# Perceiver kernel, stage 9: the 16-head cross attention two heads at a time, in two groups of 64 rows

## The reference

```python
q = split_heads(hidden_states @ q_w.T + q_b)      # 16 heads of 16 channels
k = split_heads(context @ k_w.T + k_b)            # 4096 keys
v = split_heads(context @ v_w.T + v_b)
scores = einsum('bhqd,bhkd->bhqk', q, k) / sqrt(16)
scores = where(mask, -inf, scores)
probs = softmax(scores, axis=-1)
ctx = einsum('bhqk,bhkd->bhqd', probs, v)         # heads side by side, no output product
x = x + ctx
```

## Time and profile before

| | us |
|---|---|
| median of 3 runs | 1701.7 (1700.82 to 1702.98) |
| the profiled execution | 1701.72 |
| its span in the trace | 1699.9 |
| stage 9 in it, from its first instruction to the first product of stage 10 | about 927 to 1413 |
| from the first score of stage 9 to its last sum | 962.4 to 1408 |

### The profile page before, as it was taken

The page is one execution under the profiler, slowest core; times in us unless marked ns, Lnnn a source line. Parts: engine busy times, 40 slices in busy tenths (PEclk is TensorE's granted clock), DMA queues, the critical chain, the costliest instruction groups (busy, mean ns, idle before and its releaser), DMA issues.

```text
span 1699.9 us, 21512 instructions
## 1 busy us (share of the span) xinstructions
PE 1570.8 (92%) x8708; PEld 951.9 (56%) x8708; DVE 812.7 (48%) x1515; ACT 624.1 (37%) x1177; POOL 139.7 (8%) x181
## 2 busy tenths in 40 slices
PE   7998899999999999998989799999999998678698
PEld 3676554454677554676545355555555554444597
DVE  5543530003433433333632566777788863755432
ACT  1222321012342323333422466666667773103111
POOL 0001200001000301001010412102210000000000
PEclk9999899999999999999999999999999999778699
DMA  9024133200035201122131554547654315100050
GB/s 377 16 99 160 61 106 112 74 22 17 3 105 197 64 0 33 50 98 92 42 149 30 111 90 87 99 78 194 179 91 70 60 18 211 50 1 1 1 198 13
DMA packets 40133, 147.04 MB, mean 86 GB/s; under 512 B 6073, under 2 KB 21689, under 8 KB 30777
## 3 DMA queue, kind: packets, MB, share of 16 engines
q1 hardware_dynamic: 40034, 145.67, 29.8%
HBM read 123.08 MB, written 22.56 MB: 86 GB/s over the span
## 4 chain that ended last, share of the span: by engine, by line
PE 85%; DVE 7%; ACT 5%; issue 2%; DMA 1%; SPq 0%; DVEq 0%; ACTq 0%
PE PS L157 53%; PE PS L1767 7%; PE PS L1744 7%; PE PS L1699 6%; PE PS L559 2%; PE PS L1188 2%; ACT AR L1851 1%; PE PS L1365 1%; PE PS L1198 1%; PE PS L1758 1%; PE PS L2192 1%; PE PS L2128 1%; ACT CT L1411 1%; DVE SM L2224 1%; ACT L261 1%
## 5 line engine op out<-in xcount | busy, mean ns | idle before, releaser
L1784 DVE TENSOR_REDUCE SM<-PS 128x1 f32<-128x1024 f32 x256 | 308.6, 1221 | 104.5 <-PE PS L1699 103.3
L157 PE MATMUL PS<-CN,AR 128*128 128x256 f32 x768 | 180.5, 379 | 0.0
L157 PE MATMUL PS<-CT,HT 128*128 128x512 f32 x384 | 176.5, 593 | 2.0 <-ACT HT L663 2.0
L157 PE MATMUL PS<-HT,AR 128*128 128x512 f32 x328 | 160.5, 642 | 15.1 <-ACT HT L331 10.4
L157 PEld LDWEIGHTS PS<-CN,AR 128*128 128x128 f32 x768 | 143.6, 190 | 43.9 <-issue 28.7
L1744 PE MATMUL PS<-AR 99*128 99x256 bf16 x1024 | 161.5, 275 | 6.4 <-ACT CN L410 2.4
L1699 PE MATMUL PS<-AR 97*128 97x512 bf16 x512 | 152.9, 380 | 4.3 <-DMA AR<-rows 2.8
L157 PE MATMUL PS<-AR 128*128 128x512 f32 (+3 forms) x472 | 149.2, 471 | 7.0 <-DVE AR L594 2.5
L1851 ACT ACTIVATE AR<-PS 128x512 f32<-128x512 f32 x256 | 138.1, 597 | 25.8 <-PE PS L1744 25.8
L1744 PEld LDWEIGHTS PS<-AR 99*128 99x128 bf16 x1024 | 79.0, 97 | 109.7 <-issue 35.9
L157 PEld LDWEIGHTS PS<-AR 128*128 128x128 f32 x472 | 85.3, 196 | 71.0 <-issue 53.5
(11 more groups left out here) (310 smaller groups left out, 1936.6 us busy)
## 6 DMA issues: line engine op xcount, KB each, us to landing
CN<-ctx_n SPq DMA_DIRECT2D x24, 1024.0 KB, 4.8
AR<-k_parts SPq DMA_DIRECT2D x192, 128.0 KB
k_parts<-CN SPq DMA_DIRECT2D x32, 384.0 KB, 5.9
CN<-pack SPq DMA_DIRECT2D x6, 2048.0 KB, 7.3
v_ones<-CN SPq DMA_DIRECT2D x32, 288.0 KB, 3.4
CT<-ctx_t SPq DMA_DIRECT2D x8, 1024.0 KB, 19.2
AR<-pack SPq DMA_DIRECT2D x16, 512.0 KB, 3.7
AR<-pack SPq DMA_DIRECT2D x3, 2048.0 KB, 7.3
```

The costliest lines, as they stand in the source:

```text
L157: last = te.matmul(o, l, r, start=first and k == 0, stop=final and k == n - 1, skip_group_check=True)
L1784: ve.tensor_reduce(MX9[:, n % 2, u // 4, u % 4:u % 4 + 1], PS[:, b:b + 2, :].rearrange("p a b -> p (a b)"), AX, ALU.max).then_inc(*dv.inc( ...
```

## The change

It is confined to stage 9 and to where stages 10 and 11 keep their buffers (CT and CN change places).

- The unit is a **pair** of heads: one head in rows 0 to 63, the other in rows 64 to 127. The six products are in two groups of rows: M, 49 rows per head (parts 0·0, 1·0, mask, 0·1), and R, 50 rows per head (0·1 or 2·0 and so on, and the two parts of the maximum). `QQ9[:, pair, 0]` and `KM9` hold M, `QQ9[:, pair, 1]` and `KR_9` hold R.
- `best` multiplies the M rows alone: 2 matmuls of 512 columns over 49 rows for one head. A score needs two matmuls that add up, M and then R.
- 16 pairs x 8 groups = 128 groups; a group does what two steps did. `best_beside` issues a head's `best` between the score matmuls of the other head, twice per group; `both` issues the scores of both heads of the next step in alternation, and takes its two banks before its first matmul. A group then is: 2 x `best_beside`, `both`, the mixes of the group before. `best` runs 10 groups (20 reductions) ahead, where it ran 12 steps ahead.
- `PT9` has 6 buffers. `finish` and `turn_rows` come once per pair; on VectorE the two copies of `turn_rows` stand between the two reductions of the next group.
- The 27 jobs come whole, one at the end of a group. The fetches are 12 to 16 transfers per pair, M rows 3 pairs ahead into 4 buffers and R rows 2 pairs ahead into 3; those of pair 0's M rows are issued in stage 8. The values of the second batch take the place of the first's.

```diff
+        AHEAD = 10
...
+            for u in range(2 * AHEAD):
+                if u in (0, 2, 6, 10):
+                    yield "select", (0, 2, 6, 10).index(u), 0
+                if u > 2 and u % 2 and jobs:
                     yield ("job", *jobs.pop(0))
...
+        def pair_steps():
+            for g in range(128):
+                p, k = g // 8, g % 8
+                yield "score", g, 0
+                if g:
+                    yield "mix", g - 1, 0
+                if g in PAIR_JOBS:
+                    yield ("job", *PAIR_JOBS[g])
+                if k == 2 and p:
+                    yield "finish", p - 1, 0
+                if k == 5 and p < 15:
+                    yield "best_rows", p + 1, 0
+                if k == 6 and p < 15:
+                    yield "turn_rows", p + 1, 0
...
+            def score_bank(p, s, e):
+                b, before = SR9.take(("st", 9, p, s, e), ("e", 9, p, s, e))
+                pe.wait_ge(*before, ("kr", p), ("mrow", 9, p))
+                return b
...
+            def best_beside(g, e, p, s):
+                b, bs = best_bank(g, e), score_bank(p, s, 1 - e)
                 for y in range(2):
+                    z = best(g, e, b, y)
+                    score(p, s, 1 - e, bs, y, 0)
+                    last = score(p, s, 1 - e, bs, y, 1)
+                z.then_inc(*pe.inc("best", "best_ps", 9, g, e))
+                last.then_inc(*pe.inc("score", "st_ps", 9, p, s, 1 - e))
+
+            def both(p, s):
+                ba, bb = score_bank(p, s, 0), score_bank(p, s, 1)
+                for y in range(2):
+                    score(p, s, 0, ba, y, 0)
+                    score(p, s, 1, bb, y, 0)
+                    a = score(p, s, 0, ba, y, 1)
+                    b = score(p, s, 1, bb, y, 1)
...
                 if what == "score":
+                    p, s = n // 8, 2 * (n % 8)
+                    if n + AHEAD < 128:
+                        best_beside(n + AHEAD, 0, p, s)
+                        best_beside(n + AHEAD, 1, p, s)
+                    else:
+                        both(p, s)
+                    both(p, s + 1)
...
+            for what, n, k in pair_steps():
+                if what == "score":
+                    if n + AHEAD < 128:
+                        best(n + AHEAD, 0)
+                    if rows is not None:
+                        turn_rows(rows)
+                        rows = None
+                    if n + AHEAD < 128:
+                        best(n + AHEAD, 1)
```

More of the change, by code:

```diff
@@ L1649, in start_steps @@
                     yield "best_rows", 0, 0
-                if u == 9:
+                if u == 17:
                     yield "turn_rows", 0, 0
             assert not jobs
[L1654 to L1680, removed]
@@ L1703, in turn_rows, with best_bank @@
-            def turn_rows(n):
-                b, before = SR9.take(("rows", n), ("mrow", 9, n))
-                pb = PS[:, b, 0:128].bitcast(BF16)
[L1706 to L1714, removed]
+            def best_bank(g, e):
+                b, before = BP9.take(("best", 9, g, e), ("best", 9, g, e))
+                pe.wait_ge(*before, ("km", g // 8), ("qm", g // 8 % 8))
+                return b
@@ new lines, in score @@
+            def score(p, s, e, b, z, rest):
+                _, pr, cols = of_pair(p)
+                rows, keys = (R_ROWS[e], KR_9[p % 3]) if rest else (M_ROWS[e], KM9[p % 4])
+                c = 2 * s + z
+                return te.matmul(PS[:, b, z * 256:z * 256 + 256], keys[rows, c * 128:c * 128 + 128],
+                                 QQ9[rows, pr, rest, cols], start=not rest, stop=bool(rest), skip_group_check=True)
+            def best_beside(g, e, p, s):
+                b, bs = best_bank(g, e), score_bank(p, s, 1 - e)
+                for y in range(2):
+                    z = best(g, e, b, y)
[3 more added lines that the diff above has]
+                last.then_inc(*pe.inc("score", "st_ps", 9, p, s, 1 - e))
@@ L1715, in select @@
+            def select(n):
+                m, kind = n // 2, n % 2
+                got = [PB4.take(("sel", kind, 4 * m + k), ("qr" if kind else "qm", 4 * m + k)) for k in range(4)]
+                pe.wait_ge(*[p for _, before in got for p in before], ("p0", 9, "q", m), ("p1", 9, "q", m),
+                           ("p2", 9, "q", m) if kind else None)
+                parts = ((2, 2), (3, 1), (4, 0)) if kind else ((0, 0), (1, 1))
+                for c, (piece, part) in enumerate(parts):
                     for k, (b, _) in enumerate(got):
@@ L1732, in pe_9 @@
                 if what == "best":
-                    best(n, k)
+                    b = best_bank(n, k)
+                    best(n, k, b, 0)
+                    best(n, k, b, 1).then_inc(*pe.inc("best", "best_ps", 9, n, k))
                 if what == "turn_rows":
                     turn_rows(n)
-            for what, n, k in head_steps():
+            for what, n, k in pair_steps():
                 if what == "score":
[L1738 to L1751, removed]
+                    p, s = n // 8, 2 * (n % 8)
[5 more added lines that the diff above has]
+                    both(p, s + 1)
+                if what == "job":
+                    job_pe(pe, SR9, n, k)
                 if what == "turn_rows":
@@ L1803, in dve_9, with turn_rows @@
+            def turn_rows(p):
+                _, pr, cols = of_pair(p)
+                dv.wait_ge(("row_ps", 9, p), ("qr", pr))
+                for e in range(2):
+                    r = slice(64 * e + 32, 64 * e + 34)
+                    ve.tensor_copy(QQ9[r, pr, 1, cols], bank("rows", p)[:, 0:128].bitcast(BF16)[r, :]).then_inc(
+                        *dv.inc("turn", "mrow", 9, p))
             turn_out(dv, 9, "ht", HT, 0)
@@ L1807, in dve_9 @@
                 split_d_dve(dv, (9, "q", m), QP9[:, 0, m, :], RT9[m])
[L1808 removed]
+            rows = None
+            for what, n, k in start_steps():
                 if what == "best":
```

346 lines of the change are left out of this document (196 added, 150 removed).

## The result

| | before | after |
|---|---|---|
| median, us | 1701.77 (1700.82 to 1702.98), 4 runs | 1739.17 (1736.24 to 1743.42), 4 runs |
| ratio after / before | | 1.0221, 95% interval 1.0199 to 1.0244 |
| profiled execution, its span | 1701.72, 1699.9 | 1739.7, 1737.9 |
| first exponential of stage 9 | 963.75 | 977.41 |
| last sums matmul of stage 9 | 1407.48 | 1446.68 |

Of the 38.0 by which the spans differ, 1.1 arise before stage 9, 12.6 in its start, 25.5 between the first exponential and the last sums, and 1.2 are given back behind them. So the start came out nearly as forecast (+11.5), and the loop did not (+3.0 by the terms of the prediction).

What follows compares the result with a forecast made beforehand. TensorE was taken to limit stage 9 before, a loop through ScalarE after. Groups 0, pairs +4.2, jobs +1.6, start +11.5 and wait for keys -2.8 made +14.5 on 1701.7: 1716 us, range 1688 to 1738.

Steps and rivals of the forecast that it cites:

- the start: Start of stage 9: 20 reductions instead of 12 before the first score, which comes near 973.9 instead of 962.37; +11.5 us.
- the loop: Stage 9 behind its start: groups 0, once-per-pair work +4.2, jobs +1.6, vanished wait for keys -2.8 us.
- the period of a group: Stage 9's loop through ScalarE: 2.41 lengthened by 0.42 to 2.83 us, with best or without; change 0 over 128 groups.
- The stall at the turned rows: Group after turn_rows: both waits for a bank VectorE holds, starting at 2.57 instead of 1.29; 14 pairs, 17.9 us.
- pairs: Work once per pair instead of per head: finish, turn_rows and the new stall sum to 30.8 against 26.6; +4.2 us.
- jobs: The 27 jobs in the heads: each adds 1.72, a turn of 0.09 and about 0.06 of delay, against 1.81; +1.6 us.
- the DMA wait: TensorE's wait for keys at 970.7 goes, as the third pair is needed only some 20 us later; -2.8 us.
- the longer lead: Best's lead over the scores: nothing of its cost returns at the end, groups with and without best taking 2.83 alike.
- B: Rival, stage 9's loop: period shorter than 2.83, VectorE binds at 2.64 a group; 1676, half the gain 1696; chance 0.21.
- C: Rival, best_beside: matmuls of unlike length in the two halves don't overlap; period 3.26, +51 us, 1767; chance 0.08.
- D: Rival, no change: start costs only +5.5 and VectorE's turn does half the harm; 1701; chance 0.14.
- The forecast's upper end: Top of the range, 1738: period 0.15 longer (+19) should a 64-row stream run 5 to 7% below two at once.

Runs made afterwards that it cites:

- e9: The changed kernel, but both takes its second bank only behind the first head's four matmuls; ratio to the kernel before 1.0159.
- e11: e8 with the edit of e9 (second bank of both taken behind the first head's matmuls); ratio to the kernel before 1.001.
- e3: The changed kernel with mixes between the second best_beside and both, and turned rows copied before VectorE's first reduction; ratio to the kernel before 1.006.
- e2: The changed kernel with VectorE copying the turned rows before the next group's first reduction instead of after it; ratio to the kernel before 1.0129.
- e7: The changed kernel with maxima searched 12 groups ahead instead of 10; ratio to the kernel before 1.0247.
- e5: e2 with a group's two mixes apart: best_beside, mix, best_beside, mix, both; ratio to the kernel before 1.0088.
- e8: e5 with ScalarE copying a pair's sums before the next group's third exponential instead of behind the fourth; ratio to the kernel before 0.9997.
- e4: The changed kernel with both issuing one head's four matmuls, then the other's, instead of alternating; ratio to the kernel before 1.0256.

## Why the prediction was wrong in its size

**The failed step is the period of a group.** The prediction had 2.41 + 0.42 = 2.83 and from it a change of 0 over the loop. The mechanism holds: the earlier trace rows's loop through ScalarE, lengthened by four matmuls on either side of the exponential, is what the chain shows, with best and without. Its size was off, 2.98, that is 128 x 0.15 = 19 us, more than the whole forecast. The terms: 0.04 until the first exponential (0.68, where 0.43 + 0.21 had been put together from full-row matmuls); 0.09 between the exponential's end and both; 0.02 in both. The largest, 0.09, is 11.5 of the 19 us. The 0.05 had been taken from the earlier trace rows, where the program waits for one bank before two matmuls; in the new kernel two waits stand before `both`. The traces narrow the cause to this. It is not ScalarE, and not the 64-row halves as such: behind ScalarE's exponential it is 0.05 in e9 and e11, with one wait before one head's matmuls, and behind VectorE's copy (1368.55 + 0.61 = 1369.16, to 1369.22) it is 0.06 in the same two halves. It is 0.14 in after and in e3, where the wait that ends last is an instruction of its own before the weight load. No run changed the number or the order of the waits alone, so this is read from the traces and not shown by an experiment. A loop that closes 128 times asks for each of its links to a hundredth, and three of them were borrowed from a place with another tiling and fewer waits.

**A term that was missing: the clock.** The stall at the turned rows was priced as a wait. In five pairs TensorE's granted clock also fell to 0.50 behind it (0.90 in the mean of 17 us); they are over by 1.1 to 1.3 each, 6.1 us together. e2 takes the stall away, and the clock is 1.00 in the same windows.

**The sum as measured** for the stretch from the first exponential to the last sums: groups 19.2, pairs +1.3 (a pair's surplus over eight periods is 25.73 - 8 x 2.98 = 1.89, where the prediction had 2.10 in its sum; 14 x 0.21 less than its 4.2), jobs +1.0, clock +6.1, the one long pair +0.6, the DMA wait -2.8: 25.4, and the trace has 25.5.

**The start** was +11.5 and is +12.6 within the stage, 13.7 with what came before it. The first score comes at 976.33 (973.9 forecast). The layout by hand was right to 2.4 us, and all of that stands before the eleventh reduction (964.47, for about 962): the layout had no job at the lower clock, and that one alone took 2.06 more (3.78 for 1.72 at 947.95). From there VectorE runs almost without a pause to the turned rows, as laid out.

**What held.** The stall at the turned rows, 14 times, `both` 2.57 behind the group's start; e2 returns 1.13 in each of 14 pairs, 16 us of the 17.9. The jobs, 1.92 for 1.87 each. The wait for keys does not appear. Nothing of the longer lead comes back (e7). VectorE's reductions never bind in the loop.

**The rivals.** B asked for a period under 2.7. None is seen in after; e5 and e8 reach 2.69, once the mixes stand in the waits, but TensorE's own work, turns included, then binds and not VectorE. The time was there to be had, 2.2% of it, by reordering alone. C is refuted: unlike lengths start together (1366.65), and best_beside takes 0.46, not 0.64. D took the start at +5.5; it was twice that. The forecast's upper end had counted a surplus of 0.15 per group and nothing beside it. That much came, but not from the slower 64-row streams that the upper end was meant for (a best_beside takes 0.45 to 0.46, where 1024 columns in full rows take 0.44): that the sizes agree is chance. The clock came on top.

The Trainium skill (TensorEngine Tiling (Array Packing), Theoretical Speedup) promises up to a factor of 2 for a contraction of at most 64 rows. The trace agrees for the streams alone: a best_beside behind both takes 0.45 in e8 for 1024 columns in each half, which full rows do in 0.88. But the group gains only 2.85 / 2.69 = 1.06 even there. (A group of 2.38 would by the prediction's own figures have made the loop 362.2 - 128 x 2.38 = 58 us shorter, where it says some 50.) A score needs two matmuls where it needed one, so best and scores go from four blocks of 0.44 to three; and of the 0.44 so gained e8 gives back some 0.27 in turns, four of 0.11 where the kernel before has 0.17.

## What to carry to other kernels

Splitting a matmul into halves that run side by side shortens TensorE's work and lengthens every loop that goes through another engine: more matmuls stand before the first result, more behind the freed bank. Before such a change, follow the loop at a place where the old kernel already runs into it, and measure its links in the new tiling, since each hundredth counts once per turn of the loop; count the waits too, as two banks taken together put two of them before the block. Then put work that needs no bank of the ring into the wait. A stall of 1.5 us on TensorE, once per 25 to 32 us, can cost more than itself: behind 5 of 14 such stalls in after the granted clock fell, for 1.1 to 1.3 us more each.

## What the runs showed of the hardware beyond what was expected

- Matmuls in different row halves don't start in the order of the program: e4, two heads' first matmuls within 0.1 us of one another though four apart, and their last two 0.03 apart.
- A 49-row, 512-column matmul beside 256-column ones in the other half costs neither anything: best_beside takes 0.44 to 0.46 for 1024 columns in each half.
- From the end of the instruction waited for to the released matmul: 0.14 where the wait is an instruction of its own before the weight load (after and e3, behind ScalarE), 0.05 to 0.06 where it stands on the weight load (behind ScalarE in before, e9 and e11, behind VectorE in after). Read from the traces; no run changed the waits alone.
- Each turn between 64-row and 32-column work took 0.10 to 0.11 (in e8's chain a mix is 0.57, with 0.46 of work, and a block behind a mix 0.55, for 0.45 behind both).
- The granted clock fell behind a stall of TensorE of 1.5 us in 5 of 14 pairs of after (0.50 from 1264.50 to 1267.80; 0.90 in the mean of 17 us), and not in the others with the same stall. In e5, where TensorE waits for up to 1.0 us once per pair, the loop has no such fall.
